# Attention over eight units: long and short key tiles joined in pairs, pieces dealt by columns, GpSimd's casts and divisions placed elsewhere

## The chip, the cores and the metric

The program runs on one core of one Trainium2 chip. The time is the device time of one execution, in microseconds (us), and the number quoted is the median of several runs. The core has a matrix engine (TensorE, PE), three engines for elementwise work (VectorE or DVE, ScalarE or ACT, GpSimd or POOL), and SyncE (SP), which here issues the DMA transfers. The engines run each their own list of instructions in order, and wait for one another by semaphores.

## What is computed

Two layers with a layer norm behind each half: a recurrent attention and a feed-forward part, then causal softmax attention and a mixture of experts. The change is in the third of these parts, the causal attention with 16 heads of 32 over 2 batches of 1024 tokens:

```python
def _L1_attn_ref(x, qkv_w, qkv_b, out_w, out_b):
    ...
    q = _rope(q)
    k = _rope(k)
    scores = jnp.einsum('bhqd,bhkd->bhqk', q, k) / np.sqrt(D)
    causal = jnp.tril(jnp.ones((t, t), dtype=bool))
    scores = jnp.where(causal, scores, -jnp.inf)
    attn = jax.nn.softmax(scores, axis=-1)
    out = jnp.einsum('bhqk,bhkd->bqhd', attn, v).reshape(b, t, c)
    return out @ out_w.T + out_b
```

## The kernel before

**Units, steps and pairs.** `attend` works through 8 units (`UNITS`): 4 heads (`HG`) of one batch each. In a unit the keys lie across the partitions and the queries along the columns. There are two query chunks of 512 columns (`qc` 0 and 1) and key tiles of 128 (`j`); a step is one (qc, j) and does all 4 heads. Under the causal mask chunk 0 has 4 steps and chunk 1 has 8, so `NS` is 12. The last four tiles of a chunk lie on the diagonal: of such a step only the columns from `diag(s)` on are computed, so it has 512, 384, 256 or 128 columns, and the 128 columns at its start must be masked. A unit has 4608 columns in its 12 steps, for each head.

**PE's order.** Steps go in pairs (`PAIR` = 2), six to a unit; I call them pairs 0 to 5. PE does the scores of pair p (L2076, one matmul for each head and step, into one of three PSUM banks `st`), and mixed into them the "pieces" (below); then it does the sums of the pair before it: the weighted values and the denominators (L2095, `num` and `den`, each 4 heads side by side in 32 columns of the array). A **stretch** is, from here on, the time of PE from the first score of a pair to the first sum of the pair before. So a unit is six stretches S0 to S5 and six groups of sums, and the sums of pair 5 come behind S0 of the next unit. I call the moment at which those sums of the last pair end the **mark** of the unit: between S0 and S1 on PE.

**Exponentials and masks.** ACT takes each score tile to `pt` (L2039); `pt` has four step buffers. GpSimd then clears the masked triangle of a diagonal step (L2012). The sums wait for both:

```python
            def pv(u, s):
                ...
                pe.wait_ge(exp_done, (u * NS + s + 1) * HG)
                if diag(s) is not None:
                    pe.wait_ge(masked, u * DIAGS + diags(s) + 1)
```

**Pieces.** The softmax needs the row maxima of the scores. For the next unit, and the one after it, `Maxima` computes the scores once more the other way round: 48 pieces a unit (12 for each head, of 128 to 512 columns), a matmul on PE (L1372) into one of three banks and a reduction on DVE (L1384 and L1387). `pieces_at` deals them to the steps: four to each step of a unit in the steady state. After pair 4 the maxima are turned (L1397), negated on ACT and DVE, and stored as two rows beside the next unit's queries.

**GpSimd.** Beside the masks it divides `num` by `den` (`divide`, four instructions, L1988 to L1993) for both chunks, and narrows three weight pieces of the expert stage to bf16 (`narrow`, L2213), all from buffers that SP fills (L2207). Its list is written by step: in `before`, the division of the last unit's chunk 1 and the three casts stand at step 4, and the division of this unit's chunk 0 stands at step 10. A cast waits until its load has landed, and everything behind it in GpSimd's list waits with it.

```python
    def narrow(self, pool, n):
        s = n % self.BUFFERS
        pool.wait_ge(self.loaded[s], (n // self.BUFFERS + 1) * DMA)
```

**SP.** For units 1 to 5 SP first waits until all sums of the unit before are done (the mark), since the queries, keys and values of unit u + 2 go into that unit's buffers; it then issues seven transfers of 512 KB, and behind them three stores of casts and three loads of raw weight pieces:

```python
                if u + 2 < UNITS:
                    at_least(sp, pv_done, u * NS)
                    mx.load(sp, u + 2)
```

Of the kernel before, what the change touches and what calls it, by code (L numbers as in the profile page):

```python
# [25 lines left out]
TT = TB // P  # L26
# [13 lines left out]
def alone(eng):  # L40

    eng.nop(nofuse=True)
# [1815 lines left out]
def attend(nc, a, src, dst, o_out, mx, ow, result):  # L1858
# [3 lines left out]

    ROWS = R_MAX + 2
    QC = SEQ // TB
    STEPS = [(qc, j) for qc in range(QC) for j in range((qc + 1) * TT)]
    NS = len(STEPS)
    DIAGS = sum(j >= qc * TT for qc, j in STEPS)
    PAIR = 2
    TURN_STEP, FRONT = 9, 8
    PT = 2 * PAIR  # L1870
    ST = 3
    DIVIDE_OPS = 4
# [2 lines left out]
    with Bench(nc, "at_") as b:  # L1875
# [16 lines left out]
        narrow = NarrowWeights(nc, b, a)  # L1892
        PER_UNIT = len(narrow.pieces) // UNITS
# [6 lines left out]
        def diag(s):  # L1900

            qc, j = STEPS[s]
            return (j - qc * TT) * P if j >= qc * TT else None
# [3 lines left out]

        ENDS = [s for s in range(NS) if s == NS - 1 or STEPS[s + 1][0] != STEPS[s][0]]

        def pieces_at(u, s):  # L1910

            if s <= TURN_STEP:
                begin = FRONT if u else 0
                count = NP - begin
                lo, hi = (begin + count * n // (TURN_STEP + 1) for n in (s, s + 1))
                return [(u + 1, n) for n in range(lo, hi)] if u + 1 < UNITS else []
            if u + 2 >= UNITS:
                return []
            after = NS - 1 - TURN_STEP
            lo, hi = (FRONT * n // after for n in (s - TURN_STEP - 1, s - TURN_STEP))  # L1920
            return [(u + 2, n) for n in range(lo, hi)]
# [12 lines left out]
        @block.sync  # L1934
        def _(sp):
            def store(u, qc):
                sp.wait_ge(divided, (u * QC + qc + 1) * DIVIDE_OPS)
                sp.dma_start(o_out[u * P:(u + 1) * P, qc * TB:(qc + 1) * TB], num_sb[:, qc, :])\
                    .then_inc(o_stored[qc], DMA)

            for stored in mx.v_stored:
                sp.wait_ge(stored, NB * TT // 2 * DMA)
            ow.load(sp, a)
            for u in range(UNITS):
# [3 lines that stand above are left out]
                if u == UNITS - 1:  # L1948
                    out.load(sp, 0, pv_done)
                    out.load(sp, 1, pv_done)  # L1950
                for n in range(PER_UNIT):
                    if u:
                        narrow.store(sp, (u - 1) * PER_UNIT + n)
                    narrow.load(sp, u * PER_UNIT + n)
                if u:
                    store(u - 1, 1)
                if u + 1 < UNITS:
                    mx.load_rows(sp, u + 1)
                else:
                    sp.wait_ge(pv_done, out.later_free)  # L1960
                    out.ln.load(sp, 0)
                    out.ln.load(sp, 1)
                    for n in range(PER_UNIT):
                        narrow.store(sp, u * PER_UNIT + n)
                store(u, 0)
            store(UNITS - 1, 1)
            sp.wait_ge(pv_done, UNITS * NS)
            out.load(sp, 2, pv_done)
            out.ln.load(sp, 2)
            out.ln.load(sp, 3)  # L1970
            out.load(sp, 3, pv_done)
            for qc in range(QC):
                sp.wait_ge(o_stored[qc], UNITS * DMA)
            narrow.finish(sp)
            expert_sync(sp)

        @block.gpsimd
        def _(pool):
            pool.memset(ones[:, :], 1.0).then_inc(ones_small_set, 1)
            pool.wait_ge(ones_small_set, 1)  # L1980
            mx.set_ones(pool, SLOTS - 1)
            pool.wait_ge(mx.ones_set, SLOTS)

            def divide(u, qc):

                n = u * QC + qc
                pool.wait_ge(near_ready, 2 * n + 2)
                pool.tensor_tensor(den_sb[:, qc, :], den_sb[:, qc, :], near[:, :], ALU.mult).then_inc(divided, 1)  # L1988
                pool.wait_ge(divided, n * DIVIDE_OPS + 1)
                pool.tensor_scalar(den_sb[:, qc, :], den_sb[:, qc, :], -1.0, 2.0, ALU.mult, ALU.add).then_inc(divided, 1)  # L1990
                pool.tensor_tensor(num_sb[:, qc, :], num_sb[:, qc, :], near[:, :], ALU.mult).then_inc(divided, 1)
                pool.wait_ge(divided, n * DIVIDE_OPS + 3)
                pool.tensor_tensor(num_sb[:, qc, :], num_sb[:, qc, :], den_sb[:, qc, :], ALU.mult).then_inc(divided, 1)  # L1993

            for u in range(UNITS):
                for s in range(NS):
                    if u and s == TT:
                        divide(u - 1, 1)
                    if s == TT:
                        for n in range(PER_UNIT):  # L2000
                            narrow.narrow(pool, u * PER_UNIT + n)
                        if u == UNITS - 2:
                            ow.high(pool)
                    if s == TURN_STEP + 1:
                        divide(u, 0)
                    if diag(s) is None:
                        continue
                    pool.wait_ge(exp_done, (u * NS + s + 1) * HG)
                    part = pt[:, s % PT, :, diag(s):diag(s) + P]
                    alone(pool)  # L2010

                    pool.affine_select(out=part, in_=part, compare_op=ALU.is_ge, fill=0.0, base=0,  # L2012
                                       pattern=[[0, HG], [1, P]], channel_multiplier=-1).then_inc(masked, 1)
            divide(UNITS - 1, 1)
            expert_gpsimd(pool)
# [52 lines left out]
        def _(pe):  # L2068
            def scores(u, s):
                qc, kt = STEPS[s]  # L2070
                off = diag(s) or 0
                j = u % SLOTS
                pieces = pieces_at(u, s)
                for h in range(HG):
                    at_least(pe, exp_done, (u * NS + s) * HG + h + 1 - ST)
                    pe.matmul(st[(s * HG + h) % ST][:, off:TB], kp[j][0:ROWS, h, kt * P:(kt + 1) * P],  # L2076
                              qp[j][0:ROWS, h, qc * TB + off:(qc + 1) * TB], start=True, stop=True)\
                        .then_inc(scores_done, 1)
                    for of, n in pieces[len(pieces) * h // HG:len(pieces) * (h + 1) // HG]:
                        mx.piece(pe, of, of % SLOTS, of // SLOTS, n)  # L2080

            def pv(u, s):
                qc, kt = STEPS[s]
                off = diag(s) or 0
# [3 lines that stand above are left out]
                if kt == 0:  # L2088
                    at_least(pe, copied, (u * QC + qc) * 2)
                    mx.wait_v(pe, u)  # L2090
                first, last = kt == 0, s in ENDS
                for total, lhs in ((num, None), (den, ones)):
                    for h in range(HG):
                        rows = slice(h * HD, (h + 1) * HD)
                        mm = pe.matmul(total[rows, off:TB], vv[u % SLOTS][:, kt, rows] if lhs is None else lhs[:, :],  # L2095
                                       pt[:, s % PT, h, off:TB], start=first, stop=last, skip_group_check=True)
                mm.then_inc(pv_done, 1)
# [56 lines left out]
def layers(nc, a, mixed, src, dst, result):  # L2154
    def scratch(name, shape, dt=F32):
        return nc.dram_tensor(name, shape, dt, kind="Internal").ap()

    q_parts = [scratch(f"q_{n}", [UNITS * P, SEQ]) for n in ("hi", "lo")]
    k_parts = [scratch(f"k_{n}", [UNITS * P, SEQ]) for n in ("hi", "lo")]
    v = scratch("v_tokens", [UNITS, SEQ, P])  # L2160
    o = scratch("attended", [UNITS * P, SEQ])
    with Bench(nc, "mx_") as b:
        b.ctx.callback(b.clear)
        mx = Maxima(b, q_parts, k_parts, v)
        opening(nc, a, mixed, src, q_parts, k_parts, v, mx)
        with Bench(nc, "ow_") as c:
            c.ctx.callback(c.clear)
            ow = OutWeights(c)
            attend(nc, a, src, dst, o, mx, ow, result)
# [1093 lines left out]
```

## Time and profile before

| what | us |
|---|---|
| median of three runs | 1510.72 |
| lowest and highest | 1508.88, 1512.7 |
| the profiled execution, its own time | 1510.53 |
| its span, first to last instruction | 1508.7 |
| attention stage within the span | 904.0 to 1225.7 |
| PE busy over the span | 97% |

The profiled execution is 0.19 us from the median of the runs, and 1.8 us of its time lie outside the span. The attention stage is eight units. Times in the rows further down count from the start of the span.

### The profile page before, as it was taken

To read this page: it belongs to the slowest core of one execution; us is meant where nothing else is said; L and a number is where in the kernel's file an instruction comes from. 1 tells how busy PE (TensorE), PEld (TensorE's weight loads), DVE (VectorE), ACT (ScalarE), POOL (GpSimd) and SP (SyncE) were. 2 spreads that over 40 slices of the span, in tenths; PEclk is the share of its full clock that TensorE was granted. 3 is DMA by queue.
4 is the path that set the end of the run, shared out by engine and by line. 5 is a ranking of instruction groups with operands and counts; after the bars stand their busy time and mean duration, and the time that the engine had idled before them with its cause. 6 is when DMAs were issued, how large, how long until landed. Compare 5 with 4: busy or idle time off the path is not lost. (4 is left out here: it accounts for less than half of the span.)

```text
span 1508.7 us, 22471 instructions
## 1 busy us (share of the span) xinstructions
PE 1458.7 (97%) x7696; PEld 1077.8 (71%) x7696; DVE 918.8 (61%) x1833; ACT 621.4 (41%) x1095; POOL 545.0 (36%) x455
## 2 busy tenths in 40 slices
PE   7999989999999999999999999999999999999987
PEld 6788778788888888888888775555555457777554
DVE  6887887855544654554343566666666238667664
ACT  5343455613421441342122115665566636442544
POOL 1233233302430441242053223344446557104773
PEclk9999999999999999999999998999999999999999
DMA  6121447503320531232355787666664634844336
GB/s 218 33 63 63 159 161 247 195 19 126 97 84 0 167 97 42 84 97 91 128 178 176 225 249 192 184 188 178 191 185 188 221 139 173 315 187 136 103 103 240
DMA packets 105227, 223.38 MB, mean 148 GB/s; under 512 B 9328, under 2 KB 35312, under 8 KB 104240
## 3 DMA queue, kind: packets, MB, share of 16 engines
q1 hardware_dynamic: 101392, 211.96, 43.2%
q0 software_dynamic: 3744, 10.23, 2.2%
q8 instruction: 54, 0.88, 0.3%
q14 instruction: 37, 0.30, 0.1%
HBM read 157.54 MB, written 64.36 MB: 147 GB/s over the span
## 5 line engine op out<-in xcount | busy, mean ns | idle before, releaser
L969 POOL TENSOR_TENSOR ff_w_lo<-ff_raw,ff_w_hi 128x1024 fp32r<-128x1024 f32 x64 | 153.8, 2403 | 220.9 <-ACT ff_w_hi L999 206.7
L2039 ACT ACTIVATE at_pt<-at_st 128x512 f32<-128x512 f32 (+3 forms) x384 | 161.4, 507 | 94.2 <-PE at_st L2076 90.9
L115 PE MATMUL op_bank<-ff_x_hi,ff_w_lo 128*128 128x512 f32 x512 | 199.9, 390 | 0.2 <-issue 0.2
L116 PE MATMUL op_bank<-ff_x_lo,ff_w_hi 128*128 128x512 f32 x512 | 199.7, 390 | 0.0
L117 PE MATMUL op_bank<-ff_x_hi,ff_w_hi 128*128 128x512 f32 x512 | 199.6, 390 | 0.0
L1239 DVE TENSOR_TENSOR ff_h_lo<-ff_hf,ff_h_hi 128x512 f32 (+1 forms) x64 | 146.9, 2295 | 53.8 <-ACT ff_h_hi L1127 53.6
L1384 DVE CUSTOM_DVE_ANT_0 mx_mx<-mx_mx,mx_mask 128x128 f32<-128x128 f32 (+2 forms) x200 | 100.8, 519 | 28.3 <-PE mx_mx L1372 27.3
L999 ACT ACTIVATE ff_w_hi<-ff_raw 128x1024 fp32r<-128x1024 f32 x64 | 67.8, 1061 | 118.5 <-PE op_bank L117 116.1
L2076 PE MATMUL at_st<-mx_qp,mx_kp 98*128 98x512 f32 (+3 forms) x288 | 106.1, 391 | 7.5 <-ACT at_pt L2039 4.2
L115 PEld LDWEIGHTS op_bank<-ff_x_hi,ff_w_lo 128*128 128x128 f32 x512 | 96.5, 188 | 20.8 <-issue 0.6
L117 PEld LDWEIGHTS op_bank<-ff_x_hi,ff_w_hi 128*128 128x128 f32 x512 | 96.4, 188 | 20.2
L116 PEld LDWEIGHTS op_bank<-ff_x_lo,ff_w_hi 128*128 128x128 f32 x512 | 96.4, 188 | 20.2
L115 PE MATMUL mx_mx<-ff_down_hi,ff_h_lo 128*128 128x512 f32 x256 | 100.3, 392 | 0.0
L117 PE MATMUL mx_mx<-ff_down_hi,ff_h_hi 128*128 128x512 f32 x256 | 99.8, 390 | 0.0
L116 PE MATMUL mx_mx<-ff_down_lo,ff_h_hi 128*128 128x512 f32 x256 | 99.6, 389 | 0.0
L1231 DVE SCALAR_TENSOR_TENSOR ff_hf<-op_bank,ff_sc,ff_hf 128x512 f32<-128x512 f32 x64 | 48.0, 750 | 72.3 <-PE op_bank L117 71.6
L2076 PEld LDWEIGHTS at_st<-mx_qp,mx_kp 98*128 98x128 f32 x288 | 55.8, 196 | 41.6 <-ACT at_pt L2039 17.7
L2095 PE MATMUL at_den<-at_pt,at_ones 128*32 128x512 f32 (+3 forms) x768 | 81.5, 496 | 0.0
L1372 PE MATMUL mx_mx<-mx_kp,mx_qp 96*128 96x512 f32 (+1 forms) x208 | 77.2, 373 | 3.2 <-DMA mx_kp<-k_lo 1.2
L1120 ACT ACTIVATE ff_hf<-op_bank,ff_sc 128x512 f32<-128x512 f32 x64 | 44.0, 687 | 82.7 <-PE op_bank L117 82.7
L1565 POOL TENSOR_TENSOR qkv_part_lo<-qkv_whole,qkv_part_hi 128x512 fp32r<-128x512 f32 x32 | 42.7, 1335 | 86.5 <-ACT qkv_part_hi L1580 78.6
L226 POOL TENSOR_SCALAR ff_ln_rstd<-ff_ln_mv 128x1 f32<-128x1 f32 (+1 forms) x7 | 2.0, 281 | 190.5 <-DVE ff_ln_mv L205 142.9
(471 smaller groups left out, 3405.2 us busy)
## 6 DMA issues: line engine op xcount, KB each, us to landing
ff_raw<-in_Wug SPq DMA_DIRECT2D x64, 512.0 KB, 3.6
at_raw<-in_expert_gu SPq DMA_DIRECT2D x16, 704.0 KB, 12.3
mx_qp<-q_hi SPq DMA_DIRECT2D x12, 512.0 KB, 6.6
mx_kp<-k_hi SPq DMA_DIRECT2D x12, 512.0 KB, 10.8
at_raw<-in_expert_d SPq DMA_DIRECT2D x8, 768.0 KB, 13.9
expert_gu_bf<-at_cast SPq DMA_DIRECT2D x16, 352.0 KB, 11.3
ex_e_gu<-expert_gu_bf SPq DMA_DIRECT2D x8, 704.0 KB, 8.4
tm_ln_res<-in_x SPq DMA_DIRECT2D x4, 1024.0 KB, 5.4
```

The costliest lines, as they stand in the source:

```text
L115: pe.matmul(out, cut_l(ll), cut_r(rh), start=first, stop=False, **kw)
L116: pe.matmul(out, cut_l(lh), cut_r(rl), start=False, stop=False, **kw)
L117: return pe.matmul(out, cut_l(lh), cut_r(rh), start=False, stop=last, **kw)
L969: pool.tensor_tensor(w[j][1][:, :, :, :], raw[:, j], f32(w[j][0][:, :, :, :]), ALU.subtract)\
L999: act.activation(w[j][0][:, :, :, :], raw[:, j], ACT.Copy).then_inc(w_hi_ready, 1)
L1231: dve.scalar_tensor_tensor(hf[:, j, :], up[j][:, :], sc[:, UP, bass.ds(n + j, 1)], hf[:, j, :], ALU.mult, ALU.mult).then_inc(hf_ready, 1)
L1239: dve.tensor_tensor(h_lo[:, bass.ds(n + j, 1), :], hf[:, j:j + 1, :], f32(h_hi[:, bass.ds(n + j, 1), :]), ALU.subtract).then_inc(h_lo_read ...
L1372: pe.matmul(bank[:, 0:hi - lo], self.qp[j][0:R_MAX, h, qt * P:(qt + 1) * P], self.kp[j][0:R_MAX, h, lo:hi], start=True, stop=True).then_in ...
L1384: dve.tensor_tensor_reduce(piece, piece, self.mask[:, TB - (hi - lo):], 1.0, -3e38, ALU.add, ALU.max, out)\
L2039: act.activation(pt[:, s % PT, h, off:TB], st[(s * HG + h) % ST][:, off:TB], ACT.Exp, scale=SCALE).then_inc(exp_done, 1)
L2076: pe.matmul(st[(s * HG + h) % ST][:, off:TB], kp[j][0:ROWS, h, kt * P:(kt + 1) * P], qp[j][0:ROWS, h, qc * TB + off:(qc + 1) * TB], start= ...
L2095: mm = pe.matmul(total[rows, off:TB], vv[u % SLOTS][:, kt, rows] if lhs is None else lhs[:, :], pt[:, s % PT, h, off:TB], start=first, sto ...
```

## The change

`STEPS` gets another order: in chunk 0 the tiles come as 0, 3, 1, 2 and in chunk 1 as 0, 7, 1, 6, 2, 5, 3, 4. The columns of the six pairs were 896, 384, 1024, 1024, 896, 384; they are now 640, 640, 640, 768, 896, 1024. The diagonal steps were 0 to 3 and 8 to 11; they are now 0, 1, 2, 3, 5, 7, 9, 11. The pieces were 8 to a pair; in the steady state they are now 7, 7, 7, 8, 9, 10. On GpSimd the first cast moves from step 4 to step 6, the other two to step 8, and the division of chunk 0 from step 10 to step 8, behind the casts.

```diff
-    STEPS = [(qc, j) for qc in range(QC) for j in range((qc + 1) * TT)]
+    STEPS = [(0, j) for j in (0, 3, 1, 2)] + [(1, j) for j in (0, 7, 1, 6, 2, 5, 3, 4)]
...
-    TURN_STEP, FRONT = 9, 8
+    TURN_STEP, FRONT = 9, 10
+    SHARES = (4, 3, 4, 3, 4, 3, 4, 4, 5, 4)
...
-                lo, hi = (begin + count * n // (TURN_STEP + 1) for n in (s, s + 1))
+                lo, hi = (begin + count * sum(SHARES[:n]) // sum(SHARES) for n in (s, s + 1))
...
-                    if u and s == TT:
+                    if u and s == 2 * PAIR:
                         divide(u - 1, 1)
-                    if s == TT:
-                        for n in range(PER_UNIT):
+                    if s == 3 * PAIR:
+                        narrow.narrow(pool, u * PER_UNIT)
+                    if s == 4 * PAIR:
+                        for n in range(1, PER_UNIT):
                             narrow.narrow(pool, u * PER_UNIT + n)
+                        divide(u, 0)
                         if u == UNITS - 2:
                             ow.high(pool)
-                    if s == TURN_STEP + 1:
-                        divide(u, 0)
                     if diag(s) is None:
                         continue
```

On GpSimd, in a unit of the steady state, from the three casts on, the kernel before has this (`at_pt` is the masked buffer; x6 stands for the masks of steps 10 and 11 and of steps 0 to 3 of the next unit):

```order
L2213 CAST at_cast<-at_raw 128x1408 x2
L2213 CAST at_cast<-at_raw 128x1536
L2012 AFFINE_SELECT at_pt<-at_pt 128x4x128 x2
L1988 TENSOR_TENSOR at_den_sb<-at_den_sb,at_near 128x512
L1990 TENSOR_SCALAR at_den_sb<-at_den_sb 128x512
L1991 TENSOR_TENSOR at_num_sb<-at_num_sb,at_near 128x512
L1993 TENSOR_TENSOR at_num_sb<-at_num_sb,at_den_sb 128x512
L2012 AFFINE_SELECT at_pt<-at_pt 128x4x128 x6
```

The same stretch of GpSimd's list in the changed kernel, from the mask of step 5 on (the x6 are now the masks of steps 9 and 11 and of steps 0 to 3 of the next unit):

```order
L2014 AFFINE_SELECT at_pt<-at_pt 128x4x128
L2215 CAST at_cast<-at_raw 128x1408
L2014 AFFINE_SELECT at_pt<-at_pt 128x4x128
L2215 CAST at_cast<-at_raw 128x1408
L2215 CAST at_cast<-at_raw 128x1536
L1989 TENSOR_TENSOR at_den_sb<-at_den_sb,at_near 128x512
L1991 TENSOR_SCALAR at_den_sb<-at_den_sb 128x512
L1992 TENSOR_TENSOR at_num_sb<-at_num_sb,at_near 128x512
L1994 TENSOR_TENSOR at_num_sb<-at_num_sb,at_den_sb 128x512
L2014 AFFINE_SELECT at_pt<-at_pt 128x4x128 x6
```

One mask, that of step 7, now stands behind the first cast. The next, that of step 9, stands behind all three casts and the division, where before two masks stood between the casts and the division.

On PE, around the second half of S0 of a unit and the sums of the last pair of the unit before it, the kernel before has this (`at_st` banks take scores, `mx_mx` and `at_mx` pieces):

```order
L2076 MATMUL at_st1<-at_qp2,at_kp2 128x384
L1372 MATMUL mx_mx1<-mx_kp0,mx_qp0 128x128
L2076 MATMUL at_st2<-at_qp2,at_kp2 128x384
L1372 MATMUL at_mx2<-mx_kp0,mx_qp0 128x256
L2076 MATMUL at_st0<-at_qp2,at_kp2 128x384
L1372 MATMUL mx_mx0<-mx_kp0,mx_qp0 128x384
L2076 MATMUL at_st1<-at_qp2,at_kp2 128x384
L1372 MATMUL mx_mx1<-mx_kp0,mx_qp0 128x512
L2095 MATMUL at_num<-at_pt,mx_vv1 32x256 x4
L2095 MATMUL at_den<-at_pt,at_ones 32x256 x4
L2095 MATMUL at_num<-at_pt,mx_vv1 32x128 x4
L2095 MATMUL at_den<-at_pt,at_ones 32x128 x4
```

The changed kernel has this in the same place:

```order
L2078 MATMUL at_st1<-at_qp2,at_kp2 128x128
L2078 MATMUL at_st2<-at_qp2,at_kp2 128x128
L1372 MATMUL mx_mx0<-mx_kp0,mx_qp0 128x384
L2078 MATMUL at_st0<-at_qp2,at_kp2 128x128
L1372 MATMUL mx_mx1<-mx_kp0,mx_qp0 128x512
L2078 MATMUL at_st1<-at_qp2,at_kp2 128x128
L1372 MATMUL at_mx2<-mx_kp0,mx_qp0 128x512
L2097 MATMUL at_num<-at_pt,mx_vv1 32x512 x4
L2097 MATMUL at_den<-at_pt,at_ones 32x512 x4
L2097 MATMUL at_num<-at_pt,mx_vv1 32x512 x4
L2097 MATMUL at_den<-at_pt,at_ones 32x512 x4
```

The second step of S0 has 128 columns and three pieces in place of 384 and four, and the sums behind S0 have 1024 columns in place of 384.

## Rows read from the trace of the kernel before

**Rows 1.** The page's first part: busy time and share of the span.

```profile
PE 1458.7 (97%) x7696; PEld 1077.8 (71%) x7696; DVE 918.8 (61%) x1833; ACT 621.4 (41%) x1095; POOL 545.0 (36%) x455
```

**Rows 2.** The chain of waits, from unit 3's mark to unit 4's: start, length, what.

```profile
1034.19 0.32 PE at_st L2076
...
1037.85 1.00 PE at_num L2095 x8
...
1041.00 0.43 PE at_st L2076
...
1044.75 0.57 PE at_num L2095 x8
...
1046.19 0.43 PE at_st L2076
...
1050.28 0.99 PE at_num L2095 x8
...
1053.85 0.43 PE at_st L2076
...
1057.59 1.00 PE at_num L2095 x8
...
1061.16 0.21 PE mx_mx L1397
...
1064.80 0.99 PE at_num L2095 x8
...
1066.65 0.65 PE at_num L2095 x8
...
1067.94 0.43 PE at_st L2076
...
1071.99 0.57 PE at_num L2095 x8
...
1073.42 0.32 PE at_st L2076
```

**Rows 3.** The timeline of GpSimd in unit 3: start, length, line, idle before and releaser.

```profile
1056.64 1.36 POOL L2213 CAST at_cast<-at_raw 128x1408 bf16<-128x1408 f32 x1 [13.09 <-DMA at_raw<-in_expert_gu]
1059.26 1.36 POOL L2213 CAST at_cast<-at_raw 128x1408 bf16<-128x1408 f32 x1 [1.27 <-DMA at_raw<-in_expert_gu]
1062.01 1.47 POOL L2213 CAST at_cast<-at_raw 128x1536 bf16<-128x1536 f32 x1 [1.39 <-ACT at_pt L2039]
1063.43 1.22 POOL L2012 TENSOR_SCALAR_AFFINE_SELECT at_pt<-at_pt 128x512 f32<-128x512 f32 x2
1064.62 1.28 POOL L1988 TENSOR_TENSOR at_den_sb<-at_den_sb,at_near 128x512 f32<-128x512 f32 x1
...
1069.18 1.22 POOL L2012 TENSOR_SCALAR_AFFINE_SELECT at_pt<-at_pt 128x512 f32<-128x512 f32 x2
```

**Rows 4.** SP's first transfer behind unit 3's mark; then DMA busy tenths, 1028 to 1070, 40 slices.

```profile
1034.25 0.32 SPq L1333 DMA_DIRECT2D at_qp<-q_hi  x1
...
DMA  0060001999999999999999999999999501000000
```

**Rows 5.** The chain of waits: the marks of units 1 and 6, and the last sums of unit 7.

```profile
955.76 0.32 PE at_st L2076
...
1151.83 0.32 PE at_st L2076
...
1225.42 0.26 PE at_den L2095 x8
```

**Rows 6.** GpSimd's third cast in unit 2, from its timeline.

```profile
1022.38 1.47 POOL L2213 CAST at_cast<-at_raw 128x1536 bf16<-128x1536 f32 x1 [1.44 <-DMA at_raw<-in_expert_d]
```

**Rows 7.** A window in unit 7: busy and count of PE, PEld, DVE, ACT, POOL; PEclk, DMA, GB/s.

```profile
1204.00:1208.00 4.00, 4.00 (x19) 0.94 (x23) 1.11 (x3) 3.47 (x7) 0.00 (x0) 0.50 1.02 349
```

**Rows 8.** Timelines of DVE and of GpSimd around 1217 us, in unit 7.

```profile
1216.61 2.44 DVE L1817 TENSOR_TENSOR at_o_lo<-at_raw_o,at_o_hi 128x512 fp32r<-128x512 f32 x2 [1.19 <-ACT at_o_hi L1811]
...
1216.79 1.71 POOL L1988 TENSOR_TENSOR at_den_sb<-at_den_sb,at_near 128x512 f32<-128x512 f32 x1
```

## The prediction

> **What bounds the kernel now.** I read the page first. PE is busy for 97% of the span [rows 1], so the time is the length of PE's list, and the question for the attention stage is how much of that list is matmul and how much is waiting that a busy PE hides. The Trainium skill says in "Perfetto Trace Analysis", section "Identifying the Most-Contended Engine", that matmul busy time is no good measure of the distance to the limit; by that page there may be room inside the 97%, and the chain below is where this case shows it.
>
> The chain of waits gives a whole unit, from the mark at 1034.19 to the next at 1073.42 [rows 2]: 39.23 us. Its stretches are S1 3.66 (1034.19 to 1037.85), S2 3.75, S3 4.09, S4 3.74, S5 3.64 and S0 4.05 (1067.94 to 1071.99), 22.93 in all; the six groups of sums between them take 3.15, 1.44, 3.57, 3.57, 3.14 and 1.43, 16.30 in all. Five units in a row are alike: from 955.76 to 1151.83 they take 196.07, so 39.21 each [rows 5]. Two things stand out. S1 and S5 have 384 score columns, S2 and S4 have 1024, and they are equally long: what they share is eight pieces. And the sums need masks, and GpSimd is nearly late with them. It idles 13.09 us until the first cast's load lands, does the third cast at 1062.01, masks steps 8 and 9 from 1063.43, and is through with them at 1064.65 [rows 3]; PE starts those sums at 1064.80 [rows 2]. The slack is 0.15 us.
>
> The loads come late because they queue. SP's first transfer behind the mark starts at 1034.25, 0.06 us after it, and the DMA engines are then at nine tenths or more for some 24 slices of 1.05 us without a gap [rows 4]. The third cast starts 27.82 us behind the mark [rows 3]. In unit 2, whose mark is 39.2 us before 1034.19, it starts at 1022.38, 27.4 us behind [rows 6]. The amount moved and its order are the same in the changed kernel, so I take this clock over: the first cast 22.45 us behind the mark, the second 25.07, the third 27.82 [rows 3]. The Trainium skill says in "DMA: Bandwidth & Descriptors", section "Queues, rings and completion order", that each DMA engine consumes a queue's descriptors in ring order. By that rule the loads can't pass the seven transfers ahead of them; a rule by which they could would make the time that of the second rival below.
>
> **The new order of steps and pieces, taken alone.** For the stretches I use the rate of the short ones: 3.66 us for 8 pieces, 0.457 us each [rows 2]. With 7 pieces and 640 columns S1 and S2 take 3.2 each. S0, which took 4.05 with 896 columns, lies between 3.2 and 4.05; I take 3.45, nearer to the piece rate because its columns fall to 640. S3 with 8 pieces and 768 columns lies between 3.66 and 4.09: 3.9. S4 has 9 pieces: 4.15. S5 has 10: 4.6. Together 22.5 against 22.93, so the balance by itself is worth 0.4 us a unit. The sums have the same 4608 columns and come to 16.3 again. A pair of 1024 takes 3.57 and one of 384 takes 1.44 [rows 2], 3.33 ns a column and 0.15 a pair, so one of 640 takes 2.28 and one of 768 takes 2.71. Left to itself such a unit would take 38.8.
>
> **The mask of step 7.** It is in pair 3 and now stands behind the first cast. PE asks for it behind S1, sums 0, S2, sums 1, S3, sums 2, S4 and the 512 unmasked columns of step 6: 3.2 + 2.28 + 3.2 + 2.28 + 3.9 + 2.28 + 4.15 + 1.85 = 23.1 us behind the mark. It is ready at 22.45 + 1.36 for the cast [rows 3] + 0.64 for the mask + 0.1 for the semaphore = 24.55. PE waits 1.4 us. The sums of step 7, 256 columns, end at 25.4.
>
> **The mask of step 9.** This is the term of the sum. It stands behind the other two casts and the division of chunk 0. Third cast at 27.82; from there to the next instruction 1.42 (1062.01 to 1063.43); the division from 1064.62 to 1069.18, 4.56; the mask 0.64; the semaphore 0.1 [rows 3]. That makes 34.54. PE, already delayed once, comes to it at 25.4 + S5 4.6 + the 512 columns of step 8 1.85 = 31.85 and waits 2.7 us. From 34.54 on nothing covers: the sums of step 9 take 1.29 (1066.65 to 1067.94 [rows 2]), S0 3.45, the sums of pair 5 3.57. The unit ends 34.54 + 1.29 + 3.45 + 3.57 = **42.85 us** behind its mark. And since the next unit's loads begin only at the next mark, it repeats: 42.85 - 39.21 = 3.64 us for each of five units, **18.2 us**.
>
> What hides what: the first wait costs nothing in the end, since the second would take it up, and so do S1 to S5 up to 2.7 us. Moving the cast and the division ahead frees GpSimd's time behind step 9, where nobody waits. The masks of steps 11 and 0 to 3 stand behind it and wait for ACT. SP's store of the division comes earlier by its place, and no transfer of the sum is behind it. ACT and DVE queue behind PE during the waits and have time over. The negated rows are issued after the turn ahead of S5 and are wanted at S0, later than before.
>
> **The other units.** In unit 0 the stage begins at 904 and the casts aren't behind a mark; the mark of unit 1 comes at 955.76 [rows 5]. PE asks for the mask of step 9 some 8 us before that mark (S0 and the sums of pair 5), at about 948, and the casts begin at about 930. Not held; 0, give or take 1. Unit 6 has no keys or queries to load, and its stretches change their sizes but not their sum; 0, give or take 1. Unit 7 has no pieces. Its long pair now comes last, but the columns are the same. It has a stretch in which the granted clock is 0.50, the lower of the two levels, 1.2 GHz, for 4 us, with a full PE in it [rows 7]; at 2.4 GHz that work takes 2 us, and whether this comes out longer or not at all I can't say: 0, from -3 to +3. The sum is 18.2. The profiled execution's own time is 1510.53, and the median of the runs 1510.72 lies 0.19 above it, so 1510.72 + 18.2 = **1529 us**.
>
> **A rule against it and its size.** The trace shows once what happens when GpSimd and DVE get in each other's way: in unit 7 a division's first product takes 1.71 against 1.28 us while two subtractions on DVE take 2.44 [rows 3, 8]. By that rule the reductions of the pieces, which read PSUM and at most the mask, would leave the moved division alone; the trace agrees, with 1.28 in unit 3. Without that excuse, three slowed products add 3 x 0.43 = 1.3 us a unit.
>
> **Rivals.**
> - *The chain behind the landing is longer.* The division now runs beside S5's ten reductions. At 1.3 us a unit that is 6.5 us: **1535.5**. Against it: the same division ran beside S0's eight without loss. Chance 0.08.
> - *The landings don't bind, and the balance pays: faster.* PE would have to find the mask of step 9 at 3.2 + 3.2 + 3.9 + 4.15 + 4.6 + 2.28 x 3 + 2.71 + 1.85 = 30.45 us behind the mark, so the third load must be there 4.1 us earlier, by 23.7 us behind the mark, and the first by 21.0. Then each unit saves 0.4 us, or, if S0 and S3 shrink with their columns too, up to 1.2; over eight units 3.2 to 9.6. At 0.8 a unit: **1504.3**. Against it: the DMA engines have no gap to give up [rows 4]. Chance 0.06.
> - *Part of the wait goes.* The third load lands 2 us or more earlier than in these rows, or S0 comes to less than 3: 1512 to 1519, **1515**. Chance 0.11, and half of it within 0.3% of no change.
> - *The moved mask is not behind the casts* would be the change not doing what it says; the list on GpSimd shows that it is. No chance of its own.
>
> **How the numbers follow.** The forecast, with 0.75, is 1529. Its own bounds: S0 from 3.2 to 4.05, -1.3 to +3; the landing 0.4 us earlier, -2; units 0 and 6 and the end, together -4 to +4. So 1523 to 1535. For 8 in 10 I add the longer chain and some of the partial case: 1519 to 1537. A measurement of this kernel can tell about 0.3%, 4.5 us, from no change. Faster by more than that: 0.06 from the second rival, partly within, so 0.05. Within: the rest of it and half of the partial case, 0.07. Slower: 0.88.
>
> **What would show it.** In the profile after: marks 42 to 43.5 us apart in units 1 to 5, and under 39 in none of them; in the chain of waits GpSimd, with the division and the load's wait, ahead of the sums of steps 7 and 9 (or PE idle there with the mask as releaser); the third cast still 27 to 28 us behind the mark. S0 should be near 3.45, S5 near 4.6. It is wrong if the marks stay near 39 us apart; then the landing is to be looked at first. If the marks are right and the total is not, the cause is in unit 7.

## The result and the profile after

| | before | changed |
|---|---|---|
| median, us | 1510.09 (4 runs) | 1537.88 (4 runs) |
| lowest to highest, us | 1508.88 to 1512.7 | 1534.38 to 1542.58 |
| ratio to before, 95% interval | | 1.0182 (1.0152 to 1.0212) |
| profiled execution, own time, us | 1510.53 | 1535.4 |
| its span, us | 1508.7 | 1533.6 |

The change makes the kernel slower by 27.8 us, 1.8%. The sign and the place were forecast; the size was not: 18.2 us were forecast, and the measured time is 0.9 us above 1537, the upper end of the range.

The page's first part of the changed kernel reads as [rows 1] did, with a percent less for PE:

```profile
PE 1465.5 (96%) x7696; PEld 1080.4 (70%) x7696; DVE 928.1 (61%) x1833; ACT 620.8 (40%) x1095; POOL 543.1 (35%) x455
```

SP's first transfer of a unit starts 0.06 us behind the mark [rows 2, 4], so SP's timeline shows the marks of units 1 to 5. The changed kernel's:

```profile
955.91 0.33 SPq L1333 DMA_DIRECT2D mx_qp<-q_hi  x1
...
999.14 0.33 SPq L1333 DMA_DIRECT2D mx_qp<-q_hi  x1
...
1045.88 0.33 SPq L1333 DMA_DIRECT2D at_qp<-q_hi  x1
...
1089.07 0.33 SPq L1333 DMA_DIRECT2D mx_qp<-q_hi  x1
...
1132.56 0.32 SPq L1333 DMA_DIRECT2D mx_qp<-q_hi  x1
```

The stage reaches the first mark at the same time as before (955.8, [rows 5]). Then the marks are 43.23, 46.74, 43.19 and 43.49 us apart, and the fifth interval, to PE's first score behind it at 1177.50, is 45.0. Before they were 39.21. The five intervals are 25.6 us longer, and the span is 24.9 us longer: the loss lies there.

What ends last in such a unit is shown by the chain of waits of the changed kernel, from the mark of unit 1 on (start, length, what):

```profile
955.91 0.33 SPq L1333
...
968.52 15.11 DMA at_raw<-in_expert_d
983.62 0.05 issue
983.68 1.47 POOL at_cast L2215
985.14 1.26 POOL at_den_sb L1989
...
989.62 0.65 POOL at_pt L2014
990.26 0.14 issue
990.40 0.85 PE at_num L2097 x8
991.25 0.65 PE at_den L2097 x8
991.90 0.44 PE at_st L2078
...
995.50 1.00 PE at_num L2097 x8
```

Before, the chain of a unit was PE with pieces of DVE [rows 2]. Now it leaves PE at the mark, goes through SP's queue of transfers and the load of the third weight piece, and comes back through GpSimd's cast, division and mask to the sums of step 9. In this unit the third cast starts 27.83 us behind the mark, as in [rows 3]; over the five units it is 27.83, 27.19, 27.80, 28.09 and 28.01. PE's waits name the same releaser; the largest of them in the stage (total, times, longest):

```profile
PE at_num L2097 <- POOL at_pt L2014: 16.5, 10, 2.5
```

Ten waits are two for each of five units: the masks of steps 7 and 9.

Not every unit is alike, though. Windows behind the wait of unit 1, around the wait of unit 2 and at the end of the wait of unit 5 (busy of PE, PEld, DVE, ACT, POOL, then the granted clock PEclk, DMA share, GB/s):

```profile
990.00:996.00 6.00, 5.44 (x39) 3.28 (x43) 3.34 (x12) 2.96 (x8) 1.81 (x4) 1.00 0.13 46
...
1028.00:1034.00 6.00, 3.49 (x33) 1.10 (x33) 1.60 (x6) 0.70 (x2) 5.27 (x6) 1.00 0.11 44
1034.00:1040.00 6.00, 6.00 (x23) 4.16 (x15) 3.34 (x10) 3.28 (x8) 0.65 (x2) 0.52 0.01 3
1040.00:1046.00 6.00, 6.00 (x34) 1.57 (x34) 0.92 (x4) 0.11 (x1) 0.62 (x1) 0.63 0.00 0
...
1165.00:1170.00 5.00, 2.76 (x17) 0.80 (x17) 0.00 (x0) 0.00 (x0) 2.60 (x4) 0.73 0.56 157
```

In unit 2 PE is busy for 3.49 of 6 us, and right behind that the granted clock is 0.52, nearly all of it at the lower level of 1.2 GHz. S0 then takes 5.41 us, not 3.60, and the sums of pair 5 take 5.76, from 1040.08 to the mark at 1045.84, not 3.57. In unit 5 the clock falls for a shorter time, and the sums of step 9 take 2.79 us, not 1.50. In the same place of units 1, 3 and 4 the clock stayed at 1.00, although PE stood still for the same 2.5 us ahead of step 9 in all five. What decides in which unit it falls is open.

### The profile page after: what moved, and what is told of

It is laid out like the page before. It is cut to its first block and busy times, and to the rows that moved or that the text cites. A ratio compares the mean times of both kernels' runs of the same rounds, so it can differ in the third digit from the quotient of the medians.

```text
span 1533.6 us, 22471 instructions
## 1 busy us (share of the span) xinstructions
PE 1465.5 (96%) x7696; PEld 1080.4 (70%) x7696; DVE 928.1 (61%) x1833; ACT 620.8 (40%) x1095; POOL 543.1 (35%) x455
## 3 DMA queue, kind: packets, MB, share of 16 engines
q1 hardware_dynamic: 101392, 211.96, 42.6%
## 5 line engine op out<-in xcount | busy, mean ns | idle before, releaser
L2078 PE MATMUL at_st<-mx_qp,mx_kp 98*128 98x512 f32 (+3 forms) x288 | 109.2, 403 | 9.2 <-ACT at_pt L2041 5.8
L2014 POOL TENSOR_SCALAR_AFFINE_SELECT at_pt<-at_pt 128x512 f32<-128x512 f32 x64 | 40.8, 641 | 108.5 <-ACT at_pt L2041 108.3
L1565 POOL TENSOR_TENSOR qkv_part_lo<-qkv_whole,qkv_part_hi 128x512 fp32r<-128x512 f32 x32 | 42.6, 1331 | 86.8 <-ACT qkv_part_hi L1580 79.6
```

## Experiments

My theory after the result had two parts (in the expectations the theories are numbered anew for each run). One: the mask of step 9 is late, since it stands behind the third load, its cast and the division. Two: what lies beyond 43.2 us in a unit is the granted clock, which falls when PE stands still. The rivals were that the new order of steps and pieces costs the time itself, that GpSimd works slower beside DVE, and that the loads land late. Each group of runs shared its runs of the kernel before; times of before moved by up to 2 us from group to group, so the ratios count.

**The division back behind the mask of step 9.**

```diff
                         for n in range(1, PER_UNIT):
                             narrow.narrow(pool, u * PER_UNIT + n)
-                        divide(u, 0)
                         if u == UNITS - 2:
                             ow.high(pool)
+                    if s == TURN_STEP + 1:
+                        divide(u, 0)
```

> The changed kernel with the division of chunk 0 back behind the mask of step 9 (at step 10); order, pieces and casts as changed. Theory one (the mask of step 9 is late because it stands behind the third load, its cast and the division): that mask is ready 27.8 + 1.43 + 0.64 + 0.1 = 30.0 us behind the mark, before PE asks for it at 32; the 1.4 us wait for the mask of step 7 stays. Marks 40.5 us apart, 1516 to 1519 us. Theory two (the new order of steps and pieces itself costs the time, and GpSimd's waits only fill it): marks stay at 43 or more, 1532 or more. Theory three (GpSimd works slower beside DVE): the division's products show over 1.3 us.

Measured: 1518.61 us, 1.0062 (1.0040 to 1.0085). GpSimd's timeline in unit 2, whose mark is at 996.61:

```profile
1023.82 1.47 POOL L2216 CAST at_cast<-at_raw 128x1536 bf16<-128x1536 f32 x1 [1.44 <-DMA at_raw<-in_expert_d]
1025.24 0.64 POOL L2015 TENSOR_SCALAR_AFFINE_SELECT at_pt<-at_pt 128x512 f32<-128x512 f32 x1
1025.84 1.28 POOL L1989 TENSOR_TENSOR at_den_sb<-at_den_sb,at_near 128x512 f32<-128x512 f32 x1
```

The mask is done 29.3 us behind the mark and PE's wait for it is gone; what is left is five waits for the mask of step 7, 3.5 us in total. Marks are 39.9 to 41.1 apart, close to the 40.5 expected. One instruction group of 4.5 us, moved by one place in GpSimd's list, is worth about 18 us of the 28, by the two ratios. That the order costs the hold (theory two) is out, and so is a slower GpSimd: the product still takes 1.28. Of the 7.1 us by which this run's profile is longer than the one of the kernel before, the five intervals account for 5.7 and units 6 and 7 for 2.1, the rest being 0.7 shorter.

**GpSimd's new list in the kernel before.**

```diff
-                    if s == TT:
-                        for n in range(PER_UNIT):
+                    if s == 3 * PAIR:
+                        narrow.narrow(pool, u * PER_UNIT)
+                    if s == 4 * PAIR:
+                        for n in range(1, PER_UNIT):
                             narrow.narrow(pool, u * PER_UNIT + n)
+                        divide(u, 0)
...
-                    if s == TURN_STEP + 1:
-                        divide(u, 0)
```

> The kernel before with only GpSimd's list of the change (first cast at step 6, the others and the division at step 8, ahead of the masks of steps 8 and 9). Theory one: the mask of step 8 is ready 34.5 us behind the mark, PE asks at 30.6; marks 34.5 + 0.1 + 3.14 + 4.05 + 1.43 = 43.2 apart, +4.0 for each of five units: 1530 us, up to 8 more where the granted clock falls in the waits. Theory two (order and pieces cost the time): 1510.

Measured: 1537.84 us, 1.0179 (1.0162 to 1.0196), as slow as the whole change. Marks 44.6 to 45.6 us apart. That is 1.4 to 2.4 more than the 43.2 expected. In the profile the waits are 3.7 us on average, and in each of the five units the granted clock falls and the sums right behind the wait take 4.5 to 5.9 us, not 3.14; S0, which follows, takes its usual 4.0. The run's mean granted clock is 0.979, against 0.989 in the profiled kernel before. So GpSimd's list alone brings a loss of this size in the old order too.

**The changed order with GpSimd's old list.** The edit is the reverse of the one above, in the changed kernel.

> The changed kernel's order and pieces with GpSimd's list of the kernel before (all three casts at step 4, the division at step 10). The mask of step 5 then stands behind all three casts. Theory one: it is ready 30.0 us behind the mark and asked for at 17.1, marks 30.0 + 0.4 + 4.3 + 2.7 + 4.6 + 3.1 + 3.6 + 3.6 = 52.3 us apart, +13.1 each: 1575 us, up to 15 more by the clock. Theory two (the change of GpSimd's list is not what counts): within 3 us of the changed kernel, 1535 to 1541.

Measured: 1600.22 us, 1.0597 (1.0561 to 1.0632). PE's largest wait, over units 1 to 5:

```profile
PE at_num L2096 <- POOL at_pt L2013: 61.4, 5, 12.8
```

Five waits of 12.3 us on average, the 12.9 expected. But the marks are 53.9 to 55.1 apart, not 52.3: S4 behind the wait takes 6.5 us in four of five units, where it takes 4.3 at the full clock. Unit 0 is held as well, by 4.4 us, and the first mark comes 9.5 us later than before (965.24); all of this brings the run above the 1575 to 1590 expected. So the new order does need casts that stand later, since it puts a mask at step 5. The moved casts do that part; the division ahead of the mask of step 9 is what undoes it.

**The weight loads ahead of the mark.**

```diff
+                early = 0 < u < UNITS - 2
+                if early:
+                    for n in range(PER_UNIT):
+                        narrow.store(sp, (u - 1) * PER_UNIT + n)
+                        narrow.load(sp, u * PER_UNIT + n)
                 if u + 2 < UNITS:
                     at_least(sp, pv_done, u * NS)
                     mx.load(sp, u + 2)
...
-                for n in range(PER_UNIT):
+                for n in range(0 if early else PER_UNIT):
```

> The changed kernel with SP's cast stores and raw weight loads of units 1 to 5 issued ahead of the wait for the mark, so ahead of the queries, keys and values. Nothing else moves. Theory one: the casts find their loads, no mask is late, marks 38.9 us apart; 1507 to 1512 us, no gain to speak of over the kernel before since the balance is worth 0.4 us a unit. Theory two: 1532 or more, since order and GpSimd's list stay. A rival on the balance (it is worth much once the masks are free): marks at 38 or less, under 1505.

Measured: 1516.75 us, 1.0050 (1.0033 to 1.0067). The marks of units 3 and 4:

```profile
1034.99 0.32 SPq L1333 DMA_DIRECT2D at_qp<-q_hi  x1
...
1074.48 0.32 SPq L1333 DMA_DIRECT2D mx_qp<-q_hi  x1
```

All five intervals are 39.44 to 39.49, and PE waits for no mask. With GpSimd's list and the order exactly as changed, the hold is gone when the loads are there: the third cast now starts 17.1 us behind the mark. The landing is the cause of the hold. But 39.47 is more than the 39.21 of before. Freed of the masks, the new order and deal lose 0.26 us a unit, where I had given them a gain of 0.4. The rival on the balance, 38 or less, is out for this deal. The time itself missed the 1507 to 1512 expected: the five intervals account for 1.3 us of the loss, and units 6 and 7, which take 76.4 us in this profile against 73.9 before, for 2.5 more; the rest is open.

**Order and deal apart.** The run with the weights first, with eight pieces to a pair again (`FRONT` 8, equal `SHARES`):

> The run with the weights loaded first, but with eight pieces to each pair as in the kernel before; the order of steps and GpSimd's list as changed. It parts the order of steps from the dealing of pieces. If the dealing by columns brings something: marks over 39.5 us apart, 40 or so, 1518 or more. If the dealing costs and the order is neutral: marks 39.2 apart, 1513 to 1516. If the order costs: marks 39.5 still.

Measured: 1511.72 us, 0.9993 (0.9978 to 1.0008). The marks of units 3 and 4:

```profile
1034.96 0.32 SPq L1333 DMA_DIRECT2D at_qp<-q_hi  x1
...
1074.09 0.32 SPq L1333 DMA_DIRECT2D mx_qp<-q_hi  x1
```

They are 39.13 apart: the order of steps is neutral, and the deal of 7, 7, 7, 8, 9, 10 costs the 0.35 us. The stretches show how. With eight pieces each they are 3.66, 3.70, 3.97, 3.74, 3.77 and 3.97 (S1 to S5, S0), nearly all alike. Dealt, S1 and S2 fall by 0.44 and 0.22, S0 by 0.37, and S4 and S5 rise by 0.57 and 0.80.

**All casts and the division behind the last mask of the unit.** The three casts, `divide(u, 0)` and the last `ow.high` stand at the end of the unit's loop over steps; SP's list is as it was.

> The changed kernel with all three casts and the division of chunk 0 behind the mask of step 11, SP as it was. No mask of the unit stands behind a load. Theory one: no wait for a mask, marks 39.5 us apart as with the weights loaded first, 1514 to 1518 us. A rival: the masks of steps 0 and 1 of the next unit now stand behind casts and division, which begin at about 31 us and take 9 us; if they are late (they are asked for 3.2 us behind the mark), marks 40 to 41 apart and 1518 to 1523.

Measured: 1524.83 us, 1.0086 (1.0058 to 1.0113). The marks did what was expected, 39.46 to 39.49 apart, and no mask is late. The time did not. In the profiled execution the attention stage begins 3.7 us later than in the kernel before, at 907.7, ahead of the part that was edited. Units 6 and 7 take 77.2 us against 73.9. And from the last sums of unit 7 to the end it takes 288.2 us, where the kernel before takes 283.1: the casts of unit 7 now stand behind its last mask and in front of the division, the store and the expert stage that follow. Whether the late start is chance or not wasn't settled (the other profiled executions begin the stage at 904.0 to 906.8). As a place for the casts this one is no better.

**The changed kernel again, and with the waits filled.** The first is the changed kernel, for comparison on the same chip; the second adds ten matmuls without a use:

```diff
+            def fill(u):
+                j = u % SLOTS
+                pe.wait_ge(exp_done, (u + 1) * NS * HG)
+                for n in range(FILL):
+                    pe.matmul(st[n % ST][:, :], kp[j][0:ROWS, 0, 0:P], qp[j][0:ROWS, 0, 0:TB], start=True, stop=True)
...
                     for s in before[1]:
+                        if s == TURN_STEP and 0 < u < UNITS - 2:
+                            fill(u)
                         pv(before[0], s)
```

> The changed kernel once more, to be compared with the next run on the same chip. 1534 to 1542 us; marks of units 1 to 5 are 43.2 to 43.5 us apart where PE's granted clock stays at 1.00 and 45 or more where it falls behind a wait for the mask of step 9. If the surplus over 43.2 has another cause than the clock, long units appear with the clock at 1.00 throughout.

> The changed kernel with ten extra score matmuls (98x512, results unused, about 2.2 us) on PE between the sums of step 8 and of step 9 in units 1 to 5, where it waits for the late mask. Theory one (the part of the loss beyond 43.2 us a unit is the clock that falls because PE stands still): the waits are filled, no unit shows a clock under 1.00, all five marks are 43.2 to 43.6 apart, the lowest time stays near 1534 and the median falls to 1533 to 1536. Theory two (long units are due to something else, such as loads that land late): long units remain, the median stays at 1537 to 1540. Theory three (the extra work itself counts): every unit grows by up to 2.2 us, 1545.

Measured: the changed kernel 1541.30 us (1539.80 to 1543.43), with the filler 1532.88 (1527.19 to 1538.19); against the kernel before 1.0192 (1.0168 to 1.0217) and 1.0151 (1.0123 to 1.0179). Windows around the wait of unit 2, of the changed kernel again, and below of the one with the filler:

```profile
1027.00:1033.00 6.00, 3.48 (x31) 1.10 (x33) 1.68 (x6) 0.77 (x2) 5.35 (x6) 1.00 0.11 44
1033.00:1039.00 6.00, 6.00 (x27) 4.23 (x21) 3.39 (x10) 3.28 (x8) 0.69 (x2) 0.53 0.01 3
```

```profile
1026.00:1032.00 6.00, 5.93 (x36) 3.04 (x38) 2.28 (x9) 1.38 (x3) 5.83 (x7) 1.00 0.04 12
1032.00:1038.00 6.00, 5.84 (x43) 3.24 (x39) 3.84 (x12) 2.96 (x8) 1.43 (x3) 1.00 0.09 34
```

With extra work in the wait PE is busy for 5.93 of 6 us, and the clock stays. In that profile all five intervals are 42.6 to 43.1 (the third cast starts 27.2 to 27.7 us behind the mark, a little earlier than forecast), S0 is 3.60 to 3.62 each time, and the kernel that does more work is 8.4 us faster in the median. A late load as the cause of the long units (theory two) is out, also because the third cast is early in the changed kernel's long unit 2, 27.2 us behind its mark; so is a cost of the extra work itself. But the filler stands in units 1 to 5 alone, and the two profiles differ elsewhere too. Their spans are 14.1 us apart: 6.3 of it lies in the five intervals, and 7.1 in units 6 and 7 (80.4 against 73.4). How much of the 8.4 in the medians the filled waits bring is therefore not shown. The filler doesn't cure every run: two of its five are at 1538, with a mean clock of 0.986 and 0.987 where the three faster ones have 0.991 to 0.993. Only the profiled one could be looked into. The Trainium skill describes the pattern in "TensorE: Matmul & The Clock Gate", section "HAM oscillation — how this bites in real kernels": waits on DMA between bursts of matmuls keep taking the array back to the lower clock. The traces here agree in part: 0.52 behind the wait of unit 2 and 1.00 behind the filled one, but also 1.00 behind equally long waits of other units.

**Was the kernel before already held?** The weights first, in the kernel before:

> The kernel before with the cast stores and raw weight loads of units 1 to 5 issued ahead of the wait for the mark. Tests whether the 0.15 us by which its masks of steps 8 and 9 were early is a slack or already a bound. If the landing was not a bound: marks 39.2 apart, no change. If it was: marks under 39.1.

Measured: 1511.71 us, 0.9992 (0.9976 to 1.0009), marks 39.21 to 39.25 apart. The 0.15 us that its masks were early was slack, and all that stood between it and the hold.

**Two other deals.** Both with the weights first.

```diff
-    TURN_STEP, FRONT = 9, 8
+    TURN_STEP, FRONT = 9, 6
+    SHARES = (5, 3, 3, 4, 4, 3, 4, 4, 4, 6)
```

> The same, and the pieces of the kernel before dealt as 5, 3, 3, 4, 4, 3, 4, 4, 4, 6 over steps 0 to 9 and 3 each over the last two, so that pair 5, whose pieces wait for the turned maxima, has six and the long pair 4 ten. By the piece rate S5 falls from 3.64 to about 2.7 and S1 to 3.2, S4 rises from 3.74 to about 4.6. Sum about 0.5 us less a unit: marks 38.7 apart, 1507 to 1510. If only the number of pieces counts, whatever the pair: marks 39.2.

```diff
-    TURN_STEP, FRONT = 9, 10
-    SHARES = (4, 3, 4, 3, 4, 3, 4, 4, 5, 4)
+    TURN_STEP, FRONT = 9, 9
+    SHARES = (5, 4, 5, 3, 4, 4, 4, 3, 4, 4)
```

> The changed order of steps and GpSimd's list with the weights loaded first and the pieces dealt 5, 4, 5, 3, 4, 4, 4, 3, 4, 4 and nine in the last pair. With pieces 7, 7, 7, 8, 9, 10 the marks were 39.5 apart, with 8 in each 39.1. If the loss lay in S4 and S5 with 9 and 10 pieces, this one (7 in pair 4, 9 in pair 5) comes to 38.5 to 39.1, 1507 to 1512; if any uneven deal costs, 39.3 or more.

Measured: the first, in the old order, 1508.22 us, 0.9975 (0.9963 to 0.9988), marks 38.75 apart; the second, in the new order, 1511.03 us, 0.9988 (0.9971 to 1.0005), marks 38.49 apart. The marks of units 2 and 3 of the first:

```profile
992.88 0.32 SPq L1333 DMA_DIRECT2D mx_qp<-q_hi  x1
...
1031.62 0.32 SPq L1333 DMA_DIRECT2D at_qp<-q_hi  x1
```

The first is faster than the kernel before by about 3.7 us, and its interval leaves 1 out; S5 with six pieces takes 2.55 us and S4 with ten 5.12. The second has the shortest units of all, but in its profile units 6 and 7 take 79.9 us together, where they take 73.9 before, with groups of sums of 4.0 to 5.3 us in them that take 2.3 to 3.6 at the full clock. So in that execution it gives back at the end what it gains in the middle, with the clock low in unit 7 though no mask was late in units 1 to 5.

## Why the prediction was right and where it was wrong

**The landing, the hold and its place: right.** The third cast was put at 27.82 us behind the mark and starts at 27.83 in unit 1; the mask of step 9 was to be there for PE at 34.54, and PE starts at 34.55. All three rivals with a chance have fallen: the division's product takes 1.28 beside S5's ten reductions, the landings bind, and no load landed 2 us early. The wait for the mask of step 7 was put at 1.4 us and is 0.8 on average; as forecast, it costs nothing, since the wait for step 9 takes it up. (The bounds that I listed for the forecast add up to 1521.7 to 1536, a little more than the 1523 to 1535 that I wrote.) The two runs that take away one link each, the division or the late load, take the hold away, and the run with GpSimd's list alone brings it.

**Behind the mask: 0.35 us short a unit.** The sums of step 9 were put at 1.29, from a group that runs on behind another. Behind a standstill they take 1.50 (990.40 to 991.90). S0 was put at 3.45, nearer to the piece rate than to its columns; it takes 3.60. So an undisturbed unit is 43.2, not 42.85, and five make 1.8 us.

**The clock: the step that failed.** I priced each wait by its own length, and said of the waits only what they would hide. The sum has no term for the clock behind them. I had the clock in the text for unit 7 alone, with -3 to +3, because [rows 7] shows it there. The same row should have made me ask what PE would do behind five new standstills of 2.7 us. An interval at the full clock is the start of the third cast plus 15.4 us (units 1, 3 and 4). By that, the fallen clock costs 4.15 us in unit 2, hidden in part by a load that landed 0.6 early, and 1.59 in unit 5: 5.7 together, and the landings of all five units come to -0.1. So the account of the profiled execution is 18.2 + 1.8 + 5.7 - 0.1 = 25.6, the five intervals.

The profiled execution, at 1535.4, lies inside my range; the median of 1537.88 does not. The last 2.5 us between the two were not located. The four runs with a mean clock of 0.989, 0.988, 0.985 and 0.981 took 1535.4, 1534.4, 1540.4 and 1542.6 us, so the two slowest had more of the low clock. The one slower execution with a profile, 1541.3 in the second comparison, lost the same 5.7 us to the clock in units 1 to 5 (4.2 in unit 2, 1.5 in unit 4), and what it takes beyond the first profiled execution lies in units 6 and 7 (80.4 us against 73.4). So the missing term is shown with its size; that it alone carries the median past the range is not.

**The balance: the wrong sign, and it didn't matter.** I gave the new order and deal a gain of 0.4 us a unit by a rate of 0.457 us a piece. That the number of pieces sets the length was read too easily: I took S2 and S4 of the kernel before for 1024 columns each, but S4 has 896, and the other stretch of 1024 is S3, which takes 4.09 us with the same eight pieces. Nor do columns and pieces together fix a stretch: S0 has as many of both as S4 and takes 4.05, not 3.74. S1 was right (3.2, measured 3.22), S5 too (4.6, 4.57). S2 takes 3.48 against 3.2, S4 4.31 against 4.15, S3 3.99 against 3.9. The deal costs 0.35 and the order gives 0.1. As long as the units were held, only S0 of this counted.

**The other units.** Unit 0: 0 forecast, 0.1 measured (first mark at 955.85 against 955.76). Units 6 and 7 together take 73.4 us in the profiled execution against 73.9 before, +1.35 and -1.8. The first is a miss: I said that unit 6's stretches would change their sizes and not their sum, but its S5 has no pieces, and takes 3.65 us with 1024 columns against 2.23 with 384. In the profile of the second comparison they take 80.4, with granted clocks between 0.57 and 0.79 for 24 us of unit 7, which is 6.5 more than before, where I had allowed +1 for unit 6 and +3 for unit 7. The nine profiles with the new order have 73.3 to 80.4 us for these two units, the four with the old order 72.4 to 76.0. The clock also falls in unit 7 in runs in which no mask of units 1 to 5 is late, those with the weights first among them. What decides there between the two is open: no experiment touched unit 7.

## What to carry to other kernels

Where an engine's list holds both work that others wait for and work that waits for a transfer, every item that is put behind the transfer inherits its landing; count the chain from the landing to the waiting engine before moving anything in between, even an item that itself waits for nothing. Price a new standstill of the matmul engine with the clock behind it, not by its length alone, and look for a standstill in the same trace that shows which way the clock goes. And when equal counts of small items already make stretches of different width equally long, look at what else each stretch waits for before dealing by width: here that deal cost 0.35 us a unit, while two other uneven deals gained about 0.5 and 0.6.

## What the runs showed of the hardware

- A standstill of PE of 2.5 us between full stretches let the granted clock fall in some units and not in others of the same execution: 0.52 in unit 2, 1.00 in units 1 and 3. Behind waits of 3.7 us on average (GpSimd's list in the kernel before), and behind those of 12.3 us (the old list in the new order), it fell in all five units.
- With 2.6 us of matmuls without a use inside each such wait it stayed at 1.00 through all five units of the profiled execution. The median was 8.4 us lower; a part of that may lie in units 6 and 7.
- The sums of step 9 behind a late mask take 0.2 us longer at the full clock than those that run on behind another group (1.50 against 1.29).
- The same transfers in the same order let the third cast start 27.4 to 27.8 us behind the mark in the kernel before, and 27.2 to 28.1 in the changed one.
